# Two layers on one Trainium2 core: the causal mask of attention's maximum pass moved from TensorE to VectorE

## What is computed

```python
Q = (x @ Wq + bq).reshape(B, S, Hn, Dh)            # B=1, S=4096, Hn=16, Dh=16
K = (x @ Wk + bk).reshape(B, S, Hn, Dh)
V = (x @ Wv + bv).reshape(B, S, Hn, Dh)
logits = jnp.einsum('bqhd,bkhd->bhqk', Q, K) * scale
causal = jnp.tril(jnp.ones((S, S), bool))
logits = jnp.where(causal, logits, -jnp.inf)
attn = jax.nn.softmax(logits, axis=-1)
...
gated = attn * gate[:, None, None, :]
out = jnp.einsum('bhqk,bkhd->bqhd', gated, V).reshape(B, S, E)
return out @ Wo + bo
```

## Time and profile before

| | us |
|---|---|
| median of 3 runs (3075.47 to 3087.85) | 3087.31 |
| the profiled execution, whole | 3087.55 |
| its span, first to last instruction | 3085.7 |
| TensorE busy in the span | 2676.6 (87%) |
| VectorE busy | 2270.2 (74%) |
| ScalarE busy | 1582.0 (51%) |
| attention's 2304 maximum reductions on VectorE | 1334.0 |
| attention's 9216 score products of the maximum pass on TensorE | 1038.3 |
| attention's 2048 mask products of the maximum pass on TensorE | 168.6 |

### The profile page before, as it was taken

One profiled execution on the slowest core, in us unless ns is written; L12 is line 12 of the kernel. 1 busy time (PEld: TensorE's weight loads), 2 busy tenths in 40 slices (PEclk: granted clock), 3 DMA queues, 4 the chain that ended last, 5 costly groups with the idle time before them and its releaser, 6 DMA issues. The chain is left out here.

```text
span 3085.7 us, 91077 instructions
## 1 busy us (share of the span) xinstructions
PE 2676.6 (87%) x35080; PEld 1642.8 (53%) x35080; DVE 2270.2 (74%) x4339; ACT 1582.0 (51%) x2164; POOL 374.7 (12%) x341
## 2 busy tenths in 40 slices
PE   6869999899989998999999777999977778229997
PEld 3322566666656665567556424555535555117765
DVE  3539899799979987998989705565657897775776
ACT  2320677677767776777767671111115666204442
POOL 1245000000000000000000200000002222202333
PEclk9985899999999999999999897999988888659998
DMA  4244011101111011110110001000001222313341
GB/s 139 72 98 81 3 27 27 27 5 26 26 27 26 6 26 26 27 27 5 26 26 7 6 11 55 14 27 16 11 2 45 65 72 78 112 40 108 103 112 54
DMA packets 130633, 130.27 MB, mean 42 GB/s; under 512 B 76418, under 2 KB 107780, under 8 KB 125060
## 3 DMA queue, kind: packets, MB, share of 16 engines
q1 hardware_dynamic: 124548, 120.93, 16.6%
q10 hardware_dynamic: 4224, 4.19, 0.4%
q0 software_dynamic: 1536, 0.40, 0.1%
HBM read 78.41 MB, written 46.66 MB: 41 GB/s over the span
## 5 line engine op out<-in xcount | busy, mean ns | idle before, releaser
L677 DVE TENSOR_REDUCE attn_pm<-attn_MS 128x1 f32<-128x512 f32 (+3 forms) x2304 | 1334.0, 638 | 189.1 <-PE attn_MS L721 162.1
L661 ACT ACTIVATE attn_PT<-attn_ES 128x1024 f32<-128x1024 f32 (+5 forms) x1152 | 1039.1, 951 | 372.9 <-PE attn_ES L756 370.3
L721 PE MATMUL attn_MS<-attn_KX,attn_QX 96*32 96x512 bf16 (+11 forms) x9216 | 1038.3, 375 | 11.1 <-DVE attn_pm L677 5.6
L756 PE MATMUL attn_ES<-attn_QX,attn_KX 99*32 99x512 bf16 (+8 forms) x9216 | 773.0, 362 | 51.2 <-issue 20.1
L771 PE MATMUL attn_OP<-attn_PT,attn_VH 128*17 128x512 f32 (+3 forms) x4608 | 648.5, 565 | 0.2 <-ACT attn_PT L661 0.2
L721 PEld LDWEIGHTS attn_MS<-attn_KX,attn_QX 96*32 96x32 bf16 x9216 | 411.6, 97 | 300.7 <-issue 128.3
L756 PEld LDWEIGHTS attn_ES<-attn_QX,attn_KX 99*32 99x32 bf16 x9216 | 376.6, 97 | 194.7 <-ACT attn_PT L661 55.4
L1131 PE MATMUL l0out_ring<-l0out_w,l0out_sT 128*128 128x512 f32 x512 | 224.9, 592 | 0.0
L771 PEld LDWEIGHTS attn_OP<-attn_PT,attn_VH 128*17 128x17 f32 x4608 | 189.8, 98 | 48.9 <-issue 3.1
L716 PE MATMUL attn_MS<-attn_maskb,identb 128*32 128x128 bf16 (+3 forms) x2048 | 168.6, 206 | 37.8 <-DMA attn_QX<-qk_parts 25.4
L609 POOL TENSOR_SCALAR attn_parts<-attn_nmT 32x128 bf16<-32x128 f32 x16 | 22.6, 1411 | 1387.9 <-DVE attn_nmT L686 1387.9
(11 more groups left out here) (278 smaller groups left out, 2952.9 us busy)
## 6 DMA issues: line engine op xcount, KB each, us to landing
attn_KX<-qk_parts SPq DMA_DIRECT2D x96, 128.0 KB, 6.9
attn_QX<-qk_parts SPq DMA_DIRECT2D x96, 128.0 KB, 7.6
vk_beta<-front_vk SPq DMA_DIRECT2D x8, 1024.0 KB, 3.9
kq_transposed<-front_qkG SPq DMA_DIRECT2D x8, 1024.0 KB, 4.5
delta_VK<-vk_beta SPq DMA_DIRECT2D x32, 256.0 KB, 2.8
delta_QK<-kq_transposed SPq DMA_DIRECT2D x32, 256.0 KB, 2.9
attn_out<-attn_OS SPq DMA_DIRECT2D x128, 34.0 KB
x_res<-in_L_attn_x_dram ACTq DMA_DIRECT2D x8, 512.0 KB, 8.2
```

Of the source, the lines that this page charges most:

```text
L661: nc.scalar.activation(PT[u % NPT][:, 512 - wa:512 + wb], ES[half][:, 512 - wa:512 + wb], ACT.Exp, scale=DH ** -0.5).then_inc(exp_done, 1)
L677: nc.vector.tensor_reduce(pm[r][:, i, c:c + 1], MS[slot][:, 0:w], AX.X, ALU.max).then_inc(max_taken, 1)
L721: last = nc.tensor.matmul(MS[slot][r, 0:seen], QX[b][0:ROWS, i * P + 32 * g:i * P + 32 * g + 32], KX[b][0:ROWS, 512 * c:512 * c + seen], s ...
L756: last = nc.tensor.matmul(ES[half][r, o + past:o + w], KX[b][0:MAXR, kt * P + 32 * g:kt * P + 32 * g + 32], QX[b][0:MAXR, a + past:a + w], ...
```

## The change

The mask products of the maximum pass (L716) are dropped. TensorE computes all four groups of a diagonal piece at its full width `w`. VectorE holds the mask in bf16 in a new tile `late`, 512 wide, zero but for the last 128 columns, and takes a diagonal piece with `tensor_tensor_reduce`: it adds `late[:, 512 - w:]` to the scores, writes the sum back over them in PSUM, and keeps the maximum, starting from -1e30. The other 112 pieces of a head are reduced as before. The f32 mask is loaded into the first exponential buffer `PT[0]`, which isn't in use yet, and not into a tile of its own. The masks of the attention pass (L751) stay.

```diff
-        maskf = sb("maskf", [P, 2, P]); maskb = sb("maskb", [P, 2, P], BF16)
+        maskf = PT[0][:, 0:2 * P].rearrange("p (a n) -> p a n", a=2); maskb = sb("maskb", [P, P], BF16)
+        late = sb("late", [P, 512], BF16)
...
             dve.wait_ge(mask_in, 16)
-            nc.vector.tensor_copy(maskb[:], maskf[:])
+            nc.vector.tensor_copy(maskb[:], maskf[:, 1, :])
+            nc.vector.tensor_copy(late[:, 512 - P:], maskf[:, 0, :])
+            nc.vector.memset(late[:, 0:512 - P], 0.0).then_inc(late_set, 1)
...
+            dve.wait_ge(late_set, 1)
...
                 dve.wait_ge(max_scores, count + 1)
-                nc.vector.tensor_reduce(pm[r][:, i, c:c + 1], MS[slot][:, 0:w], AX.X, ALU.max).then_inc(max_taken, 1)
+                if c == i // 4:
+                    dve.sem_inc(dheld, 1)
+                    nc.vector.tensor_tensor_reduce(MS[slot][:, 0:w], MS[slot][:, 0:w], late[:, 512 - w:], 1.0, NEG,
+                                                   ALU.add, ALU.max, pm[r][:, i, c:c + 1]).then_inc(max_taken, 1)
+                else:
+                    nc.vector.tensor_reduce(pm[r][:, i, c:c + 1], MS[slot][:, 0:w], AX.X, ALU.max)\
+                        .then_inc(max_taken, 1)
...
-                diag = c == i // 4
-                if diag:
-                    for g in range(4):
-                        r = slice(32 * g, 32 * g + 32)
-                        nc.tensor.matmul(MS[slot][r, w - P + 32 * g:w], k["identb"][:, r], maskb[:, 0, 32 * g:],
-                                         start=True, stop=False, skip_group_check=True)
                 for g in range(4):
-                    r = slice(32 * g, 32 * g + 32)
-                    seen = w - 96 + 32 * g if diag else w
-                    last = nc.tensor.matmul(MS[slot][r, 0:seen], QX[b][0:ROWS, i * P + 32 * g:i * P + 32 * g + 32],
-                                            KX[b][0:ROWS, 512 * c:512 * c + seen], start=not diag, stop=True,
-                                            skip_group_check=True)
+                    last = nc.tensor.matmul(MS[slot][32 * g:32 * g + 32, 0:w],
+                                            QX[b][0:ROWS, i * P + 32 * g:i * P + 32 * g + 32],
+                                            KX[b][0:ROWS, 512 * c:512 * c + w], start=True, stop=True)
```

More of the change, by code:

```diff
@@ L536, in attention @@
         OP = ps("OP", [P, 512])
-        held = sem("pool_held")
+        held, dheld, late_set = sem("pool_held"), sem("dve_held"), sem("late_set")
         mask_in, ready = sem("mask_in"), sem("attn_ready")
@@ L548, in _ @@
         def _(sp):
-            sp.dma_start(maskf[:], d["c_mask"].rearrange("a p n -> p a n")).then_inc(mask_in, 16)
+            sp.dma_start(maskf, d["c_mask"].rearrange("a p n -> p a n")).then_inc(mask_in, 16)
             if gate:
@@ L751, in scores @@
                             nc.tensor.matmul(ES[half][r, o:o + 32 * g + 32], k["identb"][:, r],
-                                             maskb[:, 1, 0:32 * g + 32], start=True, stop=False, skip_group_check=True)
+                                             maskb[:, 0:32 * g + 32], start=True, stop=False, skip_group_check=True)
                     for g in range(4):
```

## The result

The changed kernel takes **3112.86 us** (median of 5 runs, 3105.9 to 3115.65); the kernel before, run beside it, 3084.41 us (3075.47 to 3087.85). The ratio is 1.0091, with a 95% interval of 1.0068 to 1.0114: 28 us slower, above the range of 3076 to 3108. In the profiled execution the span grew from 3085.7 to 3111.0 us.

A forecast was written before the change was run, and what follows sets the result against it. VectorE was taken to bound the opening and head 1's start, TensorE the middles, with turns mixed. Terms +3.2 +1.1 +4.2 -6.3 = +2.2 us, on a profiled 3087.55 us, gave 3090 us, range 3076 to 3108.

The forecast's parts named there:

- What is removed: TensorE's mask products on diagonal pieces: 32 columns, 13 ns, taken as 0.02 us each, showing only in middles of heads.
- D: Extra VectorE time per diagonal piece, from the fused instruction and accumulator read: 0.07 to 0.25 us, taken as 0.10.
- The pair of ScalarE rows: ScalarE's accumulator read: the next instruction starts 0.10 us after it; basis for pricing VectorE's read.
- drained: Rival: VectorE's read is drained or costs as much, D about 0.2; +18 us, 3106 us, chance 0.20.
- two-cycle rival: Rival: fused instruction needs two VectorE cycles a column on every diagonal piece, D = 0.42; +63 us, 3151 us, chance 0.08.
- The rule that the prediction weighed: Skill's claim that VectorE's next operation doesn't start until the pipe is empty; would give the drained rival's sum.
- +3.2 opening: Head 0 alone, VectorE-bound: 32 diagonal pieces at 0.10 us each cost +3.2 us.
- +1.1 head 1's first pieces: First 22 pieces of head 1, VectorE-bound: 11 diagonal ones cost +1.1 us.
- +4.2 turns: 14 changes from one head to the next: three diagonal pieces ahead of TensorE's wait, +0.3 us each, +4.2.
- -6.3 middle: TensorE-bound middles of 15 heads: 21 diagonal pieces each, 0.02 us gained per piece, 6.3 us in all.
- The head of 91.9 us: Expected length of one head in the changed profile: 92.0 + 0.3 - 0.4 = 91.9 us.
- the faster rival: Mask products cost TensorE more than their columns (12.6 us gained), less code cuts 6 us of stops; 3077 us, chance 0.10.

The follow-up runs named there:

- dve_spread: Kernel before with only VectorE's fused instruction added (TensorE's mask products kept) and each head's twelve loads spread as six pairs over the following head: 3077.7 us.
- after_spread_pad: Changed kernel with each head's loads spread over the following head and 64 semaphore increments on TensorE's queue ahead of attention: 3066.2 us.
- after_spread: Changed kernel with each head's twelve loads spread as six pairs over the following head: 3073.1 us.
- dve_only: Kernel before with only VectorE's fused instruction added; TensorE keeps its mask products and code, so the mask is added twice: 3121.0 us.
- before_noload: Kernel before without the query and key loads inside the head loop; heads 3 to 15 compute on data of heads 0 to 2: 3065.7 us.

## Why the prediction was wrong

**What is removed: right in size, wrong in place.** 32 columns a diagonal piece, 13 ns, taken as 0.02. The middle of the head above gained 0.34 us for 21 pieces, 0.016 each, and nearly every other middle without a loop end gained 0.3. But it doesn't show only there: between dve_spread and after_spread_pad an undisturbed turn falls from 13.1 to 13.0 us, and the 14 turns, the uneven ones at the loop ends included, by 3.5 us together, where the prediction gave TensorE's part nothing.

**D, the price on VectorE: mis-sized, low side.** Forecast 0.10 us, bounds 0.07 to 0.25. From VectorE's first piece to the negated maximum the opening took 80.0 us before (227.58 to 307.6). After, TensorE's and VectorE's first rows are

```profile
228.77 1.53 PE L723 MATMUL attn_MS<-attn_KX,attn_QX 96*32 96x128 bf16 x16 [25.96 <-DMA attn_QX<-qk_parts]
```

```profile
229.28 0.30 DVE L683 CUSTOM_DVE_ANT_0 attn_MS<-attn_MS,attn_late 128x128 f32<-128x128 f32 x1 [17.72 <-issue]
```

and the maximum stands at 310.0: 80.7 us, +0.7 for 32 pieces, D = 0.02, under the lower bound. That VectorE starts 1.7 us later than before is the landing of head 0's loads, for which TensorE waits; it varies (227.83 us in after_spread). At the turn D is more: 0.19 us for the four pieces ahead of the copy, 0.05 each. The pair of ScalarE rows on which I rested D didn't carry over to VectorE's read, and the fused instruction, which also writes into PSUM, lasts at most 17 ns longer than the plain one. The drained and the two-cycle rival were both wrong. The rule that the prediction weighed (the Trainium skill, VectorE: DVE Perf Modes, "The DRAIN you can't avoid") doesn't show here either: the read starts 0.60 us after an instruction of 0.69, and the next piece starts together with the read. The section itself adds that a next operation that isn't held starts earlier, and these rows agree with that.

**The sum: near, and partly by luck.** Forecast +3.2 opening, +1.1 head 1's first pieces, +4.2 turns, -6.3 middle, together +2.2. Measured: +0.7; +0.3 (first negated maximum to first evacuation, 14.6 us before and 14.9 after); +3.2 for the turns and -2.6 for the middles, with loads spread. Together +1.6. The head of 91.9 us that I gave came out at 91.8. Every term was too big, on both sides, and the errors cancelled. The turns came close by luck as well: +4.2 was three pieces at 0.10 us; what stands behind +3.2 is 6.7 from VectorE's part, less 3.5 from TensorE's. Beyond the 0.05 us for a piece ahead of the copy, no row divides up the 6.7.

**The step that failed** is one that the sum didn't have: TensorE's stops were left as they were. I had seen the first of them and spoke of it in the faster rival alone: "fewer instructions might cut a third, 6 us". The rows gave its length and not its cause, and for this change the sign was wrong. The code did shrink, from 255 blocks to 242, and the stops grew by 14.1 us. Of the 21.7 us by which the loop grew, those are 14.1, the waits for the maxima's rows 3.2, the change itself 0.6. The 3.8 that remain are argued, not shown: I put them down to the lower clock behind the new stops. The traces bound it. From 330 us to the last negated maximum TensorE's granted clock stands at its lower level for 44 us before and 61 after; by an estimate from these 17 us at half speed, at most 8.5 us are lost.

**What stays open.** That the burst of loads and the place of the code together make the stops beyond the loop ends' own is shown: by taking the loads away, by spreading them, and by shifting the code, each in both kernels, and by the block that lands ahead of every restart. Which of the change's effects moved the fetches (TensorE's shorter code, VectorE's longer code, which comes through q14, or times that differ by a few tenths) isn't told apart; dve_only shows only that the first isn't needed. Why a fetch waits while data moves, whether in its engine's line or at memory, no run here shows either.

## What to carry to other kernels

Before you price an edit to an unrolled engine queue, look for "issue" stops and at the instruction queue around them: if blocks of code and a burst of loads meet there, the place of the code is a term of its own. Here it moved one kernel by 12 and 24 us and the other by some 40, more than a few nanoseconds per instruction came to, and an edit that left TensorE's code alone moved it too. Measure such an edit against a version in which the burst is spread, or against two or three shifts of the code; one number for before and one for after told here mostly how the lottery fell. And spread prefetches that have a whole head to arrive: here that gave 0.7%, more than the change gave anywhere.

## What the runs showed of the hardware

- VectorE's add-and-maximum over 512 columns, one operand and the result in the same PSUM slot and the other in bf16, lasts 698 ns against 685 for the plain maximum. Its accumulator read lasts 141 ns. Over the opening the two together cost 0.02 us a piece more than the plain maximum; at a turn four of them cost 0.19.
- Code arrives in blocks of 16 KB. While twelve loads of 128 KB keep the engines at 97%, no block moves for 12 us (after, 414.8 to 426.7). In the traces with the burst TensorE stops for 0.3 to 9.2 us, and all 88 stops of the fourteen traces end 1.2 to 2.2 us after a block has landed. Without the burst there are the stops at the jump back of its loop, 3.3 to 3.8 us, and few of up to 0.6 elsewhere; a head with a loop end is 7.6 us longer (before_noload).
- 128 semaphore increments ahead of attention on TensorE's queue moved the first negated maximum by 7 to 13 us (four kernels).
- A send of 8 KB that took over 2.5 us (39 of 630, up to 4.0) always had a block of code on its way beside it; without one a send took 1.7 to 2.3 us. In after_spread that cost each of four turns 0.8 us or more.
